# A convolution-and-attention block on one core: steps 1 to 4 reordered

## The reference

```
z   = layer norm of x over the channels;  g = group norm of z (32 groups)
qkv = conv1d_same(g, qkv_w, 16 taps) + qkv_b         # 256 -> 768 channels
per batch and head (4 heads of 64 channels):
  w = softmax((q * s)^T (k * s)),   h = w applied to v     # 1024 x 1024
x1  = x + z + conv1d_same(h, proj_w, 5 taps) + proj_b
t   = layer norm of x1 over the channels
out = x1 + t, with a one-hot digit addition on 32 of the channels of t
```

## Time and profile before

| what | value |
|---|---|
| median of three runs | 1137.94 us |
| profiled execution, its own time | 1135.47 us |
| span of the profiled execution | 1133.6 us |
| PE busy | 949.7 us, 84% of the span |
| PE weight load busy | 747.4 us, 66% |
| DVE busy | 739.2 us, 65% |
| ACT busy | 668.7 us, 59% |
| POOL busy | 305.2 us, 27% |
| mean granted clock of PE | 0.938 of full speed |

### The profile page before, as it was taken

How to read it: one execution, slowest core, us unless ns; L and a number is a source line. 1 busy time by engine, 2 the same in 40 slices (tenths; PEclk the granted TensorE clock), 3 DMA queues, 4 the chain that set the end, 5 groups by cost and what they waited for, 6 DMA issues and landing times.

```text
span 1133.6 us, 19565 instructions
## 1 busy us (share of the span) xinstructions
PE 949.7 (84%) x7826; PEld 747.4 (66%) x7826; DVE 739.2 (65%) x1240; ACT 668.7 (59%) x1088; POOL 305.2 (27%) x205
## 2 busy tenths in 40 slices
PE   1758378987868989887989899999999989977874
PEld 1556256766755767666666777787787767766654
DVE  6878685646444466767687556656556665777777
ACT  5646436656356656775676566657657565655632
POOL 2744440332120122343342101112111014133220
PEclk7889679998988999999999999999999999999988
DMA  7040133557437872545553635365463973543412
GB/s 265 1 166 32 47 122 87 141 123 149 132 104 177 204 188 76 141 112 121 159 122 76 149 107 115 88 169 104 94 162 89 219 174 64 112 103 75 112 56 75
DMA packets 289563, 136.23 MB, mean 120 GB/s; under 512 B 268865, under 2 KB 271297, under 8 KB 288961
## 3 DMA queue, kind: packets, MB, share of 16 engines
q1 hardware_dynamic: 289472, 134.98, 47.2%
HBM read 46.70 MB, written 16.95 MB: 56 GB/s over the span
## 4 chain that ended last, share of the span: by engine, by line
PE 35%; DVE 26%; issue 14%; ACT 14%; POOL 5%; DMA 4%; SPq 1%; ACTq 0%; POOLq 0%; DVEq 0%
PE cP L1110 8%; PE cM L1110 8%; PE cQ L1110 7%; DVE smx L1562 5%; POOL wsum L596 4%; ACT arena L987 4%; DVE W L1335 4%; DVE arena L1539 3%; PE psV L1153 2%; PE psS L1176 2%; PE psT L1176 2%; PE psV L1157 1%; ACT arena L818 1%; DVE arena L1414 1%; DMA staging<-w_qkv 1%
## 5 line engine op out<-in xcount | busy, mean ns | idle before, releaser
L1110 PE MATMUL cP<-U,W 128*128 128x256 f16 x1728 | 214.1, 284 | 34.8 <-DVE W L1335 18.3
L1110 PE MATMUL cM<-U,W 128*128 128x256 f16 x1728 | 209.9, 280 | 35.5 <-DVE W L1335 13.0
L1110 PEld LDWEIGHTS cP<-U,W 128*128 128x128 f16 x1728 | 173.8, 101 | 73.9 <-ACT y_all L871 17.6
L1110 PE MATMUL cQ<-U,W 128*128 128x256 f16 x1728 | 205.8, 276 | 18.1 <-DVE W L1335 14.1
L1110 PEld LDWEIGHTS cM<-U,W 128*128 128x128 f16 x1728 | 171.5, 100 | 73.1 <-issue 13.9
L1110 PEld LDWEIGHTS cQ<-U,W 128*128 128x128 f16 x1728 | 168.9, 98 | 52.4 <-DVE W L1335 9.2
L1539 DVE SCALAR_TENSOR_TENSOR arena<-arena,smx 128x1024 f16<-128x1024 f32 x128 | 175.1, 1368 | 9.0 <-ACT arena L1000 8.3
L1000 ACT ACTIVATE arena<-arena,smx 128x1024 f16<-128x1024 f32 x128 | 147.0, 1148 | 4.2
L632 POOL TENSOR_TENSOR ap<-ap 128x512 f32<-128x512 f32 x24 | 35.8, 1490 | 371.3 <-ACT ap L883 371.3
L980 ACT ACTIVATE smx<-smx,tiny 128x1 f32<-128x1 f32 x128 | 37.1, 290 | 155.9 <-DVE smx L1562 155.6
L1562 DVE TENSOR_REDUCE smx<-psS 128x1 f32<-128x1024 f32 x64 | 77.8, 1215 | 41.0 <-PE psS L1176 40.5
(11 more groups left out here) (201 smaller groups left out, 1258.1 us busy)
## 6 DMA issues: line engine op xcount, KB each, us to landing
staging<-w_qkv SPq DMA_DIRECT2D x28, 512.0 KB, 5.6
U<-kept_u SPq DMA_DIRECT2D x21, 520.0 KB, 4.9
U<-kept_u SPq DMA_DIRECT2D x7, 780.0 KB, 4.9
kept_u<-temp_b SPq DMA_DIRECT2D x9, 520.0 KB, 3.3
arena<-x_tok SPq DMA_DIRECT2D x8, 512.0 KB, 6.8
arena<-arena SPq DMA_DIRECT2D x16, 256.0 KB, 3.7
W<-x_tok SPq DMA_DIRECT2D x4, 1024.0 KB, 5.8
out_tok<-W SPq DMA_DIRECT2D x3, 1024.0 KB, 4.9
```

Of the source, the lines that this page charges most:

```text
L1110: last = mm(out, W[:, j, wl, c, QTAPS * (3 * family + third) + tap, :], u[:, ul, c, at + tap:at + tap + QUART], start=((g, c, t) in OPENER ...
```

## The change

Three groups of edits.

1. Batches 2 and 3: u_high moves from ACT to POOL, directly ahead of u_low of the same part. The parts come in the order 0, 1, 4, 2, 5, 3 (`u_place` counts them), the slots of parts, differences and stores are spread anew, and batch 3 moves whole into step 2.
2. Tiles 3 to 5: the six squares over 128 x 2048 elements become 24 over 128 x 512 (square_chunk), which SP loads singly into the halves of wsum, in steps 1 and 2, each behind the turn of a unit; the load of tile 3 for its preparation comes behind them. The parts of the weights are prepared in three stages: sums, then the high half at the end of the same slot (ACT_BEHIND instead of ACT_BEFORE), then the low half in the slot after.
3. In all steps: ACT does main_copy at the end of slots 1, 7, 13, and main_common_copy and heads_out ahead of the exponential; DVE does heads_sum ahead of half_y and the reciprocal.

```
@@ tables
-        BY_HALF = (0, 1, 4, 6, 8, 10, 12, 2, 3, 5, 7, 9, 11, 13)
+        BY_HALF = (0, 1, 4, 6, 10, 8, 2, 12, 3, 5, 11, 7, 9, 13)
+        U_ORDER = ((0, 1, 2, 3, 4, 5), (0, 1, 2, 3, 4, 5), (0, 1, 4, 2, 5, 3), (0, 1, 4, 2, 5, 3))
+        def u_place(b, part):
+            return SPLITS * b + U_ORDER[b].index(part) + 1
         POOL_AT = {
+            1: {0: [("ring", 0)], 5: [("u", 2, 0), ("u", 2, 1)], 7: [("u", 2, 4)], 11: [("u", 2, 2), ("u", 2, 5)], 13: [("u", 2, 3)]},
+            2: {2: [("u", 3, 0), ("u", 3, 1)], 5: [("u", 3, 4)], 7: [("u", 3, 2)], 8: [("u", 3, 5)], 11: [("u", 3, 3)]},
+            3: {1: [("sums", 3, 0)], 3: [("sums", 3, 1)], 5: [("sums", 3, 2)], 7: [("sums", 3, 3)], 9: [("sums", 3, 4)],
+                11: [("sums", 4, 0)], 13: [("sums", 4, 1)], 15: [("sums", 4, 2)], 17: [("sums", 4, 3)]},
...
+        SQUARES = [(n, i) for n in (1, 2) for i in range(4, 16)]
+        ACT_BEHIND = {
+            3: {1: [("hi", 3, 0, 1)], 3: [("hi", 3, 4, 6)], 4: [("hi", 3, 10)], 5: [("hi", 3, 8, 2)], 6: [("hi", 3, 12)],
+                7: [("hi", 3, 3, 5)], 8: [("hi", 3, 11)], 9: [("hi", 3, 7, 9)], 10: [("hi", 3, 13)],
...
+        for q, (n, i) in enumerate(SQUARES):
+            ACT_BEHIND.setdefault(n, {}).setdefault(i, []).append(("chunk", q))
         DVE_AT = {
+            1: {1: [("diff", 2, 0)], 2: [("diff", 2, 1)], 3: [("sub", 2, 0)], 6: [("sub", 2, 1)], 8: [("sub", 2, 2)], 17: [("diff", 3, 0)]},
+            2: {0: [("diff", 3, 1)], 1: [("sub", 3, 0)], 4: [("sub", 3, 1)], 6: [("sub", 3, 2)], 16: [("wadd", 3)], 17: [("wscale", 3), ("wscale", 4), ("wscale", 5)]},
+            3: {0: [("yscale", 3)], 1: [("yscale", 4), ("yscale", 5)], 2: [("lo", 3, 0, 1)], 4: [("lo", 3, 4, 6)],
+                5: [("lo", 3, 10)], 6: [("lo", 3, 8, 2)], 7: [("lo", 3, 12)], 8: [("lo", 3, 3, 5)], 9: [("lo", 3, 11)],
...
@@ SP
+            BATCH_2 = {5: 0, 6: 1, 8: 4, 11: 2, 12: 5, 13: 3}
+            BATCH_3 = {2: 0, 3: 1, 5: 4, 7: 2, 8: 5, 11: 3}
+            def load_chunk(q):
+                if q >= 2:
+                    sp.wait_ge(S["chunk_done"], q - 1)
+                else:
+                    sp.wait_ge(S["wlo_done"], PARTS * 3)
+                m, piece = 3 + q // 8, q % 8
+                c, t = piece // 4, piece % 4 * QTAPS * P
+                sp.dma_start(wsum[:, q % 2].rearrange("p k o -> p (k o)"), w_qkv[m, c][:, t:t + QTAPS * P]) \
+                    .then_inc(S[f"chunk_in{q % 2}"], 16)
...
+                    if k in (0, 1) and 3 <= u < 15:
+                        load_chunk(12 * k + u - 3)
+                    if k == 1 and u == 12:
+                        load_w(3, range(4), [("ulo_done", SPLITS * NB)])
@@ POOL
             def u_low(b, part):
+                if b >= 2:
+                    u_high(pool, b, part)
@@ u_high, now for either engine
+            if b < 2:
+                nc.scalar.activation(u_part(u, part, 0), u_source(b, part), ACT.Copy).then_inc(S["uhi_done"], 1)
+            else:
+                nc.gpsimd.tensor_copy(u_part(u, part, 0), u_source(b, part)).then_inc(S["uhi_done"], 1)
@@ ACT
+            def square_chunk(q):
+                act.wait_ge(S[f"chunk_in{q % 2}"], 16 * (q // 2 + 1))
+                a(wsum[:, q % 2], wsum[:, q % 2], ACT.Square, accum_out=chunk_sum[:, q // 8, q % 8:q % 8 + 1]) \
+                    .then_inc(S["chunk_done"], 1)
@@ ACT, the step: ahead of the scaled maximum
+                    if conv and i in (2, 8, 14):
+                        main_common_copy(n, p, i // 6)
+                    if k >= 1 and i == 1:
+                        heads_out(k - 1, 3)
+                    if attn and i in (7, 11, 15):
+                        heads_out(k, i // 4 - 1)
                     if unit:
...
-                    if conv and i in (2, 8, 14):
-                        main_copy(n, p, i // 6)
-                        main_common_copy(n, p, i // 6)
@@ ACT, the step: at its end
+                    if conv and i in (1, 7, 13):
+                        main_copy(n, p, i // 6)
+                    for entry in ACT_BEHIND.get(n, {}).get(i, []):
+                        extra(*entry)
@@ DVE, the step: behind prob_low, ahead of half_y and the reciprocal
+                    if k >= 1 and i == 1:
+                        heads_sum(k - 1, 3)
+                    if attn and i in (7, 11, 15):
+                        heads_sum(k, i // 4 - 1)
```

More of the change, by code:

```diff
@@ L367, in wait, with u_high @@
                 eng.wait_ge(S[name], value)
+        def u_high(eng, b, part):
+            u = u_home(b, part)
+            wide = part in (0, 4, 5)
+            if wide:
+                eng.wait_ge(S["sub_done"], 2 * (FAMILIES * b + max(part - 3, 0) + 1))
+            elif part > 1:
+                eng.wait_ge(S["diff_done"], 2 * b + part - 1)
+            else:
+                eng.wait_ge(S["eo_done"], (2, 4 + 2, 4 * NB, 4 * NB)[b])
+                if b >= 2:
+                    eng.wait_ge(S["edges"], 2)
+                if b == 3:
+                    eng.wait_ge(S["eo_in"], 16)
+            if b >= 2 or (b == 1 and part > 1):
+                wait(eng, "ub_out" if wide else "ua_out",
+                     16 * (FAMILIES * (b - 1) + (max(part - 3, 0) if wide else part - 1)))
+            if b < 2:
+                nc.scalar.activation(u_part(u, part, 0), u_source(b, part), ACT.Copy).then_inc(S["uhi_done"], 1)
+            else:
+                nc.gpsimd.tensor_copy(u_part(u, part, 0), u_source(b, part)).then_inc(S["uhi_done"], 1)
         def home(k):
@@ L400, in store_u @@
                 lo, hi = u_at(part)
-                sp.wait_ge(S["ulo_done"], SPLITS * b + part + 1)
+                sp.wait_ge(S["ulo_done"], u_place(b, part))
                 sp.dma_start(kept_u[b][:, lo:hi], u_home(b, part)[:, :, :, :].rearrange("p l c w -> p (l c w)")) \
@@ L503, in _ @@
                         store_u(2, BATCH_2[u])
-                    if k == 0 and u == 10:
-                        store_u(2, 5)
+                    if k == 0 and u == 14:
                         load_eo()
-                    if k == 0 and u in BATCH_3:
+                    if k in (0, 1) and 3 <= u < 15:
+                        load_chunk(12 * k + u - 3)
+                    if k == 1 and u in BATCH_3:
                         store_u(3, BATCH_3[u])
[L509 to L525, removed]
+                    if k == 1 and u == 12:
+                        load_w(3, range(4), [("ulo_done", SPLITS * NB)])
+                    if k == 2 and u in (7, 11):
+                        load_w(4, (0, 1) if u == 7 else (2, 3), [("wlo_done", PARTS * 3 + (8 if u == 7 else PARTS))])
+                    if k == 3 and u == 3:
                         load_w(5, (2, 3), [("wlo_done", PARTS * 5)])
@@ L568, in u_low @@
                 u = u_home(b, part)
-                pool.wait_ge(S["uhi_done"], SPLITS * b + part + 1)
-                pool.wait_ge(S["ulo_done"], SPLITS * b + part)
+                if b >= 2:
+                    u_high(pool, b, part)
+                pool.wait_ge(S["uhi_done"], u_place(b, part))
+                pool.wait_ge(S["ulo_done"], u_place(b, part) - 1)
                 g.tensor_tensor(u_part(u, part, 1), u_source(b, part), u_part(u, part, 0), ALU.subtract).then_inc(S["ulo_done"], 1)
@@ L748, in phase @@
                       bias=ab[:, c, 1:2], scale=ab[:, c, 0:1]).then_inc(S["eo_done"], 1)
[L750 to L767, removed]
             def w_hi(m, *parts):
@@ L786, in squares @@
             def squares(m, c):
[L787 to L797, removed]
-                a(junk, wst(m)[:, c].rearrange("p s k o -> p (s k) o"), ACT.Square,
-                  accum_out=am[:, at:at + 1]).then_inc(S["c_m"], 1)
+                wait(act, "wam_done", m)
+                weights_in(act, m, c)
+                a(W[:, m % 3, 0, c, 0:2 * PH_TAPS], wst(m)[:, c].rearrange("p s k o -> p (s k) o"), ACT.Square,
+                  accum_out=am[:, 4 + c:5 + c]).then_inc(S["c_m"], 1)
+            def square_chunk(q):
+                act.wait_ge(S[f"chunk_in{q % 2}"], 16 * (q // 2 + 1))
+                a(wsum[:, q % 2], wsum[:, q % 2], ACT.Square, accum_out=chunk_sum[:, q // 8, q % 8:q % 8 + 1]) \
+                    .then_inc(S["chunk_done"], 1)
             def extra(kind, k, *which):
@@ L804, in extra @@
                     last_stage(kind, k, *which)
-                if kind == "u":
-                    u_high(k, *which)
+                if kind == "chunk":
+                    square_chunk(k)
                 if kind == "squares":
@@ L935, in first_step @@
                 w_hi(2, 0, 1)
[L936 to L937 removed]
+                u_high(act, 1, 0)
+                u_high(act, 1, 1)
                 w_hi(2, 4, 2)
[L939 removed]
+                u_high(act, 1, 2)
                 ln_root(3)
@@ L1006, in step @@
                         qk_hi(3 * n + 1, 0, 1)
-                    if k >= 1 and i == 1:
-                        heads_out(k - 1, 3)
                     if k >= 1 and i == 2:
```

(17 more changed lines are left out.)

48 lines of the change are left out of this document (21 added, 27 removed), and 30 rows, old and new, of tables (ACT_BEFORE, ACT_BEHIND, DVE_AT, POOL_AT).

## The result

The changed kernel takes 1089.58 us (median of 4 runs, 1087.46 to 1090.35), the kernel before 1138.2 beside it: 0.9568 of it, 95% interval 0.9545 to 0.9591, or 49 us less. The forecast was 1074 us, with a range of 1056 to 1108: 64 us less was forecast, 49 measured. The profiled execution took 1090.35 us, its span 1088.6.

The account below looks back on a forecast made before the run. It took PE's idle stretches and the lower clock behind them, with DVE in step 3, as the bound. Steps 1 to 4 gave -60 us, step 8 -4: 1137.9 - 64 = 1074 us, range 1056 to 1108.

Parts of the forecast that it names:

- the ring: Steps 1 and 2: low half, piece landing, square, maximum, back to low half; 10.85 us against 10.89 for two slots.
- What bounds it: PE, busy 84% of the span; steps 1 to 4 are 82 us over step 5's floor, 60.5 of it idle PE.
- Sum by step: Steps 1 to 4 at 102, 103, 107, 102 us, together 414 against 474.2; step 8 -4, other steps 0.
- Small squares: Steps 1 and 2: 24 squares of 0.85 us, +8 us on ACT; 2 us a step for landing in crowded slots.
- a rival with a chance of 0.19: Steps 1 and 2: small loads land at 7.6 us, making slots 2.15 us longer: +38 us, 1112 us; chance 0.19.
- Group 3: All steps: PE's waits for main_copy (24.5 us) and heads_sum (17.5) in steps 1 to 4 nearly go; step 8 -4.
- the step of DVE's bound: Step 3, bound by DVE and its waits for ACT: 118.2 less 8.5 for heads_sum and 3.5 of reciprocal waits, 106 us.
- Batches 2 and 3 off ACT: Steps 1 and 2: 12 high copies leave ACT with 20.1 + 17.4 us of waits; GpSimd gets 15 us; cost 1 a step.
- Weight parts a slot apart: ACT's 34.9 us of waits for GpSimd's sums addressed; step 3 at 106 us by DVE, step 4 at 102.
- All of it: Rival: steps 1 to 4 reach the floor, -82 us, and step 8 -4: 1052 us; chance 0.10.
- Slower: Rival: piece landings in steps 1 and 2 take 10 us or more, eating up the gain; at 12 us 1164; chance 0.06.
- change their names: Rival: DVE and ACT in turn set the slot, PE stays as idle as before: 1130 to 1140 us; chance 0.05.

Follow-up runs that it names:

- e11: The changed kernel with small pieces loaded one unit earlier and the kept sequence loaded last, a repeat of e6: 1062.71 us, 0.9334 of before.
- e1: The changed kernel with each small piece of raw weights loaded one unit earlier, nothing else: 1069.86 us, 0.9391 of before.
- e2: The changed kernel without the 24 loads of small pieces, ACT doing copies with sums in place of squares: 1063.3 us, 0.9341 of before.
- e6: e1 with the kept sequence loaded behind all turns and U loads of step 1, batch 3's differences and first parts a slot later: 1064.15 us, 0.9354.
- e4: The kernel before with the third group of edits alone: 1099.93 us, 0.9656 of before.
- e3: The changed kernel with the third group of edits undone: 1123.45 us, 0.9865 of before.
- e10: The kernel of e6 with only main_copy and the common copy back behind the exponential of slots 2, 8, 14: 1068.84 us, 0.9388 of before.
- e9: The kernel of e6 with only heads_out and heads_sum back behind the high half and the reciprocal: 1095.69 us, 0.9632 of before.
- e7: e1 with the high copies of batches 2 and 3 back on ACT, in the new slots: 1073.49 us, 0.9433 of before.
- e8: e1 with each of the 12 high copies of batches 2 and 3 done twice by GpSimd: 1069.93 us, 0.9409 of before.

## Why the prediction was right, and where its terms were off

The time lies in the range, and just inside the forecast's own 1058 to 1092. Two of the steps do not bear out the forecast: it called itself wrong if a step of 1 to 4 stayed above 112 us, and steps 1 and 2 did. Nor did three more of its signs come: the waits for pieces were 2.7 us each in the mean, where over 2 meant that the ring binds; PE's waits for main_copy and heads_sum were 19.8 us, not under 8; and the clock was 0.93 and 0.96 in steps 1 and 2, not 0.98. ACT's waits for stores did go, and steps 3 and 4 came as said.

*What bounds it.* Right. Steps 1 to 4 had 82 us over the floor of step 5; the change took away 37.6 of them, e11 62.2.

*Sum by step.* Forecast 102, 103, 107, 102 and -4 in step 8; measured 114.2, 116.4, 102.0, 104.0 and -7.4. The signs of the misses differ: steps 1 and 2 together 25.6 over, step 3 5 under, step 4 2 over, step 8 3.4 under. The total is 16 us over by the medians. That 8.4 us of misses went the other way is luck, but not what saved the range: without them the time would have been some 1098.

*Small squares: the term that was mis-sized.* It was taken as 2 us a step for the ring; e1, which only loads the pieces earlier, takes 14.7 us off step 1 and 7.4 off step 2. The mechanism was the one named as a rival with a chance of 0.19, at a shorter landing: the time lies between the forecast (landing at 3.3 us) and that rival (7.6 us, 1112). The sum of 10.85 against 10.89 us had no room, and the store taken for the landing (3.25 us) was too good: the pieces take 4.1 in the median and stand behind stores in SP's queue in the slots that have one. With the 7.25 us of the instance above in place of 5.47 the ring is some 12.6 us, an estimate, and by the prediction's own rule (12.6 - 10.9) / 2 = 0.9 us a slot, 21 us over 24 slots, near the 22.1 that e1 takes off (which holds the wait behind the 2 MB load of the next paragraph too). The Trainium skill (DMA: Bandwidth & Descriptors, "Anatomy of one DMA") gives an estimate of 2.6 us for 256 KB, for DMAs issued by GpSimd; the trace has 4.1 for those of SP beside transposes, so the measurement decides, and the ring does not fit. The slack of 7 us a step did not save it: heads_out now stands behind the piece too, and PE's waits of 4.3 and 9.2 us are for heads_sum, which needs heads_out.

*Step 2: a load put at nothing.* The sum took step 2 at 103, "with the extra 2 MB load of tile 3's weights under it". In the trace of the change the longest wait of the step hangs on that load: the turn behind it takes 6.86 us to issue, the piece behind the turn comes 8.05 us late for ACT, and PE is idle for 9.25 of the 14.3 us of the step. In e1 a turn behind the same load takes 7.23 us and a piece is 5.53 us late, but heads_out no longer stands behind that piece, and PE has no such wait. No run moves this load alone, but e2 keeps it and drops the pieces, and has step 2 at 104.1: the load costs by the piece behind it. The moved load of the kept sequence, which the sum did not count, is no part of this miss (0.48 us of PE's waiting in the change); it cost 6.5 us of step 2 in e1, by e6.

*Group 3.* Right in its mechanism, but not in its sizes. Of the 24.5 + 17.5 = 42 us of PE's waits counted, steps 1 to 4 gave 29.0 with the order alone (e4) and 25.7 on top of the rest (e3); step 8 gave 8.3 and 7.8, where 4 was taken. The split was wrong too: on the kernel of e6, main_copy undone alone costs 6 and heads_out and heads_sum 33 (e10, e9). Who PE waits for names the last of a chain, not what the chain's delay is made of. A likely reading, which no run isolates, is that heads_sum held DVE, DVE's maximum held ACT, and ACT's main_copy came late by it. In the step of DVE's bound, "8 of 8.5" for heads_sum was nearly what e9 shows, 9.6.

*Batches 2 and 3 off ACT.* The waits for stores went, as said, but the reason was only half right: the new slots and order of parts did it, not the engine (e7). They went over to GpSimd, 31.8 us in steps 1 and 2, and its list had room: with twice the copies, and DVE stretched a little more, e8 took no longer.

*Weight parts a slot apart.* ACT's waits for sums fell by 29.7 us, and steps 3 and 4 by 3.9 and 1.9 us on top of the order. e4, without this part, still has 25.9 us of these waits and steps of 105.9 us. So once the order is right, little of them is on the path; with the old order steps 3 and 4 fell by 6.0 and 3.6 (e3).

*Rivals.* "All of it" did not come: steps 3 and 4 keep 4 to 6 us. "Slower" and "change their names" are out, though step 1 by itself is the second one: 37.5 us of waits for stores in steps 1 and 2 became 51.3 for pieces.

## What to carry to other kernels

An engine that serves a tight loop should first do what others wait for, and take a copy out of a bank before the long operation rather than behind it: moving eight short instructions of a step (heads_out and heads_sum, four each) was worth 33 us (e9). A load that feeds an instruction at the end of the same slot must be issued a full slot before; write its ring down (event, queue, landing, work, back to the event) and ask for some us of room in it, not for a sum that just fits. And when a large load is put or moved along a queue, look at what stands directly behind it: here a transpose, and then the small load that everything else waited for.

## What the runs showed of the hardware

A transpose by DMA took some 1.6 us to issue in most slots. It took 6.63 us directly behind a 1 MB load and a 256 KB copy (e1), 6.86 directly behind four loads of 512 KB (the change), 5.74 behind a load of U (e1), and 2.92 where the same 1 MB load was 4.9 us old (the change). What else was in flight differs between these, so they are instances and not a rule.

A copy with a change of type on GpSimd took 1.05 us for 1040 elements in a partition, as quick as ACT's for the same copy (1.05 to 1.07, before), while GpSimd's subtraction of two inputs took 2.16. DVE's low half took 1304 ns in the mean between 178 and 386 us before, with GpSimd busy 47 us there, 1443 with 66 us (e1) and 1489 with 77 us (e8).
